# VectorE writes both bias tiles of a step, one comparison makes both one-hots, and a group's two additions are split over two steps

## The reference, cut to what matters

```
edge_feat = concatenate([x[src], x[dst], edge_attr])          # per edge
h         = mish(edge_feat @ W1 + b1)
messages  = mish(h @ W2 + b2)
agg       = segment_sum(messages, dst, num_segments=1250)
```

## Time and profile before

| | us |
|---|---|
| median of 3 runs | 1094.78 (1094.32 to 1095.49) |
| the profiled execution, own time | 1094.15 |
| its span | 1092.3 |
| busy in the span: PE / PEld / DVE / ACT / POOL | 1033.1 / 871.1 / 861.9 / 884.3 / 724.6 |

### The profile page before, as it was taken

One profiled execution on the slowest core, in us unless ns is written; L12 is line 12 of the kernel. 1 busy time (PEld: TensorE's weight loads), 2 busy tenths in 40 slices (PEclk: granted clock), 3 DMA queues, 4 the chain that ended last, 5 costly groups with the idle time before them and its releaser, 6 DMA issues.

```text
span 1092.3 us, 18562 instructions
## 1 busy us (share of the span) xinstructions
PE 1033.1 (95%) x5629; PEld 871.1 (80%) x5630; DVE 861.9 (79%) x1500; ACT 884.3 (81%) x1077; POOL 724.6 (66%) x626
## 2 busy tenths in 40 slices
PE   3558999999999999999999999999999999999997
PEld 1226889998889888888888888888888888888796
DVE  7998536635526389999999999999999999999686
ACT  6985735624503799999999999999999999999584
POOL 6875438745255587777777777777777777760227
PEclk8889999999999999999999999999999999999999
DMA  2005962674276387766676666667766666761002
GB/s 106 9 1 139 181 222 73 212 242 149 77 240 116 94 177 163 162 161 139 136 147 139 139 141 146 136 141 141 147 137 138 144 146 134 142 133 39 1 1 95
DMA packets 82914, 141.63 MB, mean 130 GB/s; under 512 B 11115, under 2 KB 39020, under 8 KB 82742
## 3 DMA queue, kind: packets, MB, share of 16 engines
q0 software_dynamic: 38048, 87.58, 40.1%
q1 hardware_dynamic: 44822, 53.52, 15.3%
HBM read 115.42 MB, written 20.39 MB: 124 GB/s over the span
## 4 chain that ended last, share of the span: by engine, by line
PE 85%; DVE 7%; ACT 2%; issue 2%; POOL 1%; DMA 1%; DVEq 1%; ACTq 0%; POOLq 0%
PE banks L1149 12%; PE banks L1150 12%; PE banks L1154 12%; PE banks L1047 10%; PE banks L1181 7%; PE banks L1131 7%; PE banks L1124 6%; PE banks L1091 5%; PE banks L965 4%; PE banks L1112 4%; DVE edge_counts L1823 2%; PE banks L1244 2%; DVE key_onehot L1762 1%; PE banks L1020 1%; PE banks L1147 1%
## 5 line engine op out<-in xcount | busy, mean ns | idle before, releaser
L798 POOL DMA_INDIRECT gather_pq<-q_table,dst x157 | 326.1, 2077 | 57.2 <-issue 47.5
L790 POOL DMA_INDIRECT gather_pq<-p_table,src x157 | 174.8, 1113 | 117.7 <-PE banks L1131 66.7
L1149 PE MATMUL banks<-w_lo,h_hi 128*128 128x512 f32 x620 | 242.0, 390 | 0.0
L1150 PE MATMUL banks<-w_hi,h_hi 128*128 128x512 f32 x620 | 241.8, 390 | 0.0
L1154 PE MATMUL banks<-w_hi,h_lo 128*128 128x512 f32 x620 | 166.0, 389 | 0.0
L1154 PEld LDWEIGHTS banks<-w_hi,h_lo 128*128 128x128 f32 x620 | 116.4, 188 | 24.4
L1150 PEld LDWEIGHTS banks<-w_hi,h_hi 128*128 128x128 f32 x620 | 116.4, 188 | 23.8
L1149 PEld LDWEIGHTS banks<-w_lo,h_hi 128*128 128x128 f32 x620 | 116.4, 188 | 23.3 <-issue 0.7
L2131 DVE SCALAR_TENSOR_TENSOR h_full<-mish_work,banks 128x512 f32<-128x512 f32 (+1 forms) x154 | 98.4, 681 | 45.1 <-ACT mish_work L1465 40.8
L2156 DVE SCALAR_TENSOR_TENSOR message<-mish_work,banks 128x1024 f32<-128x1024 f32 x78 | 95.3, 1222 | 8.4 <-ACT mish_work L1489 0.3
L1124 PE MATMUL banks<-ident,gather_pq 128*128 128x128 f32 x628 | 96.5, 275 | 1.4 <-DVE h_full L2131 0.8
(11 more groups left out here) (274 smaller groups left out, 2607.6 us busy)
## 6 DMA issues: line engine op xcount, KB each, us to landing
edge_attr<-in_edge_attr_t SPq DMA_DIRECT2D x20, 256.0 KB, 2.8
attr_high<-edge_attr_hi SPq DMA_DIRECT2D x40, 128.0 KB, 2.2
attr_low<-edge_attr_lo SPq DMA_DIRECT2D x40, 128.0 KB, 1.8
edge_attr_parts<-attr_high SPq DMA_DIRECT2D x79, 64.0 KB
edge_attr_parts<-attr_low SPq DMA_DIRECT2D x79, 64.0 KB
x_nodes<-h_hi POOLq DMA_DIRECT2D x10, 256.0 KB, 14.9
x_nodes<-h_lo POOLq DMA_DIRECT2D x10, 256.0 KB, 7.9
p_table<-p_stage SPq DMA_DIRECT2D x10, 256.0 KB, 2.0
```

The costliest lines, as they stand in the source:

```text
L790: nc.gpsimd.indirect_dma_start(GP[:, 2 * j + k, :], None, p_tab[:, :], bass.IndirectOffsetOnAxis(ap=SRC[:, 2 * s + k:2 * s + k + 1], axis= ...
L798: nc.gpsimd.indirect_dma_start(GP[:, 2 * j + k, :], None, q_tab[:, :], bass.IndirectOffsetOnAxis(ap=DST[:, 2 * s + k:2 * s + k + 1], axis= ...
L1149: pe.matmul(at, h_high(s, j)[:, c, e], W2_LO[:, c, :], start=False, stop=False, skip_group_check=True)
L1150: pe.matmul(at, h_high(s, j)[:, c, e], W2_HI[:, c, :], start=False, stop=False, skip_group_check=True)
```

## The change

Four edits, all in the edge loop:

1. `b2_both_tiles` takes the place of `b2_first_tile`: VectorE copies the bias to both Z2 banks of step s with one instruction of 1024 elements. ScalarE's `b2_second_tile` goes, and TensorE's product ones times bias in odd steps. One semaphore, `b2_seeded`, takes the place of two.
2. `hots1` is one `tensor_tensor` comparison of 256 elements in place of two `tensor_scalar` comparisons of 128.
3. The addition to the low block stays at the end of the even step. The addition to the next block moves into the odd step that follows, behind its two `full1`, together with the branch `more_of`.
4. `load_range` moves from the end of the even step to the odd step, behind `message`.

```diff
@@ TensorE, z2
-                if after(s, 2) and k == 0:
-                    pe.wait_ge(b2_first, s - 1)
-                elif after(s, 2) and j == 0:
-                    pe.wait_ge(b2_second, s)
+                if after(s, 2):
+                    if k == 0:
+                        pe.wait_ge(b2_seeded, s - 1)
                 else:
                     pe.matmul(at, ONES_R[:, :], B2_R[:, :], start=True, stop=False, skip_group_check=True)
@@ ScalarE
-            def b2_second_tile(s, j):
-                nc.scalar.copy(Z2[:, 2 * j + 1, :], B2_ROW[:, 0, :]).then_inc(b2_second, 2)
...
-                if j == 1 and after(s, 3) and live(s - 1) and tiles(s - 1) == 2:
-                    b2_second_tile(s - 1, 1 - j)
...
-            act.wait_ge(b2_in, 16)
@@ VectorE
-                make_hots([ONEHOT[:, j, k, :] for k in range(2)], REL_G, 2 * s).then_inc(hot_ready, 1)
+                wide = [P, 2, P]
+                nc.vector.tensor_tensor(ONEHOT[:, j, :, :], IOTA[:, 0:P].rearrange("p (o k) -> p o k", o=1).broadcast_to(wide),
+                                        REL_G[:, bass.ds(2 * s, 2)].rearrange("p (t o) -> p t o", o=1).broadcast_to(wide),
+                                        ALU.is_equal).then_inc(hot_ready, 1)
...
-            def b2_first_tile(s, j):
+            def b2_both_tiles(s, j):
                 dve.wait_ge(msg_full, s - 1)
-                nc.vector.tensor_copy(Z2[:, 2 * j, :], B2_ROW[:, 0, :]).then_inc(b2_first, 1)
+                nc.vector.tensor_copy(Z2[:, 2 * j:2 * j + 2, :], B2_ROW[:, :, :].broadcast_to([P, 2, DIM])).then_inc(b2_seeded, 1)
...
+            def group_low(s, n, group, bank):
                 wait_extras()
                 dve.wait_ge(agg_done, SUMS1 + group)
                 dve.wait_ge(seg_done, s + 1)
-                add_sums(n, group, bank).then_inc(agg_done, 1)
+                add_low(n, group, bank)
+
+            def group_next(s, group):
+
+                add_next(0, group, SEG[:, 0, :]).then_inc(agg_done, 1)
+                more_of(s, 0, group + 1)
...
             def edge_step(s, j, i):
 
                 if live(s):
                     for h in range(2):
                         full1(s, h)
+                if j == 1 and live(s - 4):
+                    group_next(s - 4, i - 2)
...
                 if live(s - 2):
                     message(s - 2, j)
+                if j == 1 and live(s - 3):
+                    load_range(0, i - 1)
                 if live(s - 2):
                     hots1(s - 2, j)
                     if live(s):
-                        b2_first_tile(s, j)
+                        b2_both_tiles(s, j)
                 if live(s):
                     lo1(s, j)
                 if live(s - 3):
-                    sums1(s - 3, i - 2 + j, j == 0)
-                if live(s - 2) and j == 0:
-                    load_range(0, i - 1)
+                    if j == 0:
+                        group_low(s - 3, 0, i - 2, SEG[:, 0, :])
+                    else:
+                        more_of(s - 3, 0, i - 1)
@@ VectorE, behind the last step
+            group_next(FINAL - 3, EDGE_GROUPS - 3)
+            load_range(0, EDGE_GROUPS - 2)
             hi2(FINAL - 2)
```

More of the change, by code:

```diff
@@ L418, in gnn_kernel @@
         h_full = [sem(f"h_full_{h}") for h in range(2)]
-        z2_done, b2_in, b2_first, b2_second = (sem(n) for n in ("z2_done", "b2_row_in", "b2_in_first_tile", "b2_in_second_tile"))
+        z2_done, b2_in, b2_seeded = (sem(n) for n in ("z2_done", "b2_row_in", "b2_in_both_tiles"))
         b_exp, b_sq, b_ln, b_r, msg_full, msg_hi, msg_lo = (sem(n) for n in
@@ L1505, in edge_step @@
                     sq2(s - 2)
-                if j == 1 and after(s, 3) and live(s - 1) and tiles(s - 1) == 2:
-                    b2_second_tile(s - 1, 1 - j)
-                if live(s - 2):
                     log2(s - 2)
@@ L1682, in node_tile, with add_low, add_next @@
                 return AGG[:, bass.ds(nt, 1), :].rearrange("p o d -> p (o d)")
[L1684 to L1690, removed]
+            def add_low(n, row, bank):
+                at = node_tile(low_tile(n))
+                nc.vector.scalar_tensor_tensor(at, bank, FROM_LOW[:, bass.ds(row, 1)], at, ALU.mult, ALU.add)
+            def add_next(n, row, bank):
+                at = node_tile(dve.snap(range_regs[n][R_NEXT], min_val=0, max_val=NT - 1))
+                return nc.vector.scalar_tensor_tensor(at, bank, BELOW_LOW[:, bass.ds(row, 1)], at, ALU.mult, ALU.add)
             def sums_extra(n, rel, tile, hots, bank, added):
@@ L2170, in lo2 @@
                 nc.vector.tensor_tensor(MSG_LO[:, :, :], MSG[:, :, :], MSG_HI[:, :, :].bitcast(F32), ALU.subtract).then_inc(msg_lo, 1)
-            def add_group(s, n, group, bank):
+            def group_low(s, n, group, bank):
                 wait_extras()
@@ L2177, in add_group @@
                 dve.wait_ge(seg_done, s + 1)
-                add_sums(n, group, bank).then_inc(agg_done, 1)
+                add_low(n, group, bank)
+            def group_next(s, group):
+                add_next(0, group, SEG[:, 0, :]).then_inc(agg_done, 1)
+                more_of(s, 0, group + 1)
+            def add_group(s, n, group, bank):
+                group_low(s, n, group, bank)
+                add_next(n, group, bank).then_inc(agg_done, 1)
             def more_of(s, n, added):
                 sums_extra(n, REL_G, 2 * s, [XHOT_R[:, k, :] for k in range(tiles(s))], SEG[:, 1, :], SUMS1 + added)
[L2183 to L2189, removed]
             def edge_step(s, j, i):
```

## The result

The changed kernel takes 1111.45 us in the median (1110.47 to 1113.96, 4 runs), the kernel before 1095.02 beside it. The ratio is 1.0154, 95% interval 1.0135 to 1.0173: slower by 1.5%. The profiled execution took 1110.63 with a span of 1108.8; before it was 1094.15 and 1092.3.

A forecast was written before the change was run, and what follows sets the result against it. A loop through VectorE, TensorE and ScalarE was taken to set 16.74 us a pair; after the change the odd seed's loop, 5.88 + 1.22 + 0.13 + 4.85 + 5.11 = 17.19, adds 16.2 over 36 pairs, less 0.5: 1110, range 1100 to 1119.

The forecast's parts named there:

- a loop through VectorE's even step: Edge loop before the change: VectorE, TensorE and ScalarE in turn set the pair at 16.74 us; 16.15 after the change.
- TensorE's own need: Edge loop: TensorE alone would need 16.66 us a pair before, 16.43 without its bias product of 0.23.
- the loop of the odd seed: From an odd step's full1 through bias copy, TensorE and exp1 to the next odd full1: 16.04 us before, 17.19 after.
- The copy: VectorE's bias copy of 1024 elements into PSUM: bounds 0.69 and 1.22 us, 1.22 taken, 0.53 more in each step.
- The one-hots: VectorE's one comparison of 256 elements for two: 0.34 us from start to start, gain 0.05 a step, bounds 0 and 0.15.
- The register load: VectorE's 0.75 us load in the odd step: taken as hidden beside the message of 1.22, with 0.1 allowed.
- The number of pairs: Odd steps from 5 to 77: 36 pairs, 16.2 us more in all; -0.5 ahead of the first stall.
- VectorE's own order: VectorE's instructions in the changed edge loop without its idle time: 16.44 us a pair, so not what binds.
- A sign that came only half: Profile after: full1 of both steps starts as inv1 ends, VectorE idle in both; ScalarE's share falls to some 93.
- A fast copy: Rival A, bias copy: 1024 elements take 0.69 us, loop 16.66, pair 0.08 shorter, time 1092; chance 0.08.
- a hidden seed: Rival B, odd step: TensorE doesn't wait for the seed and decides; pair 16.44 us, time 1084; chance 0.09.
- a late register load: Rival C, odd step: load isn't hidden behind the message and holds the one-hots back; up to 1138 us; chance 0.11.

The follow-up runs named there:

- the kernel with the old seeds: Changed kernel, but bias written as before: VectorE tile 0, ScalarE tile 1 of even steps, TensorE's product in odd steps; 1094.30 us, ratio to before 0.9994.
- the cut copy: Changed kernel with the odd steps' wide bias copy in two, tile 1 behind lo1 with its own semaphore; 1096.21 us, ratio to before 1.0007.
- the other two kernels: Changed kernel with an extra 256-element comparison ahead of the even copy, 1112.38 us; changed kernel with one-hots behind the copy, 1103.54 us.

## Why the prediction was right

The forecast was 1110 with a range of 1100 to 1119; measured were 1111.45, and 1110.63 in the profiled execution against 1109.9. By its steps:

- **The limits before.** That TensorE's fullness hid a loop through VectorE's even step stands: with that loop shortened, in the kernel with the old seeds, the wait of line 1124 goes and the pair falls by only 0.03. TensorE's own need was put at 16.66, and about 16.65 comes out of that kernel; what holds it at 16.71 is the loop of the odd seed, 0.06 above it.
- **The copy** measures 1.220 over the loop, the upper bound that was taken. By the Trainium skill ("VectorE: DVE Perf Modes", "What auto-detection actually checks") the doubled rate for a single fp32 source needs both the source and the destination in SBUF. The trace agrees for the wide form too: 1.220 into PSUM, against 0.69 for the cast of 1024 inside SBUF.
- **The one-hots** take 0.33 from start to start (610.77 to 611.10), 0.34 was taken; their mean is 0.418.
- **The register load** is hidden: message to one-hots is 1.14 us in odd steps, with the load beside it (609.63 to 610.77), and 1.13 to 1.14 in even ones.
- **The loop of the odd seed**: 5.88, 1.22, 0.13, 4.85, 5.11 were forecast; 5.86, 1.22, 0.12, 4.88, 5.10 are there. 17.19 against 17.18 in the pair shown and 17.15 in the mean of 35.
- **The number of pairs** was right in effect: 14.6 us in 35 pairs (0.42 each, against 0.45), and 1.9 outside, where -0.5 was put down. Two small errors of opposite sign; what lies in the 1.5 us behind step 77 I have not taken apart.
- **VectorE's own order** was put at 16.44. In the timeline of the changed kernel odd to even `full1` takes 8.31 without a wait for another engine, where its starts in the kernel before, with the additions, copies and comparison put in, give 7.93 - 0.86 + 0.67 + 0.53 - 0.05 = 8.22. The even `full1` also waits for the signal of `lo1`, the instruction just ahead of it, and sits idle for 0.10 there, which the term left out. The expectation of the cut copy, which takes the idle time and gaps off the whole pair, has 16.64. So the term was too small by 0.1 to 0.2; it didn't decide.
- **A sign that came only half.** `full1` of both steps was to start as `inv1` ends, with VectorE idle ahead of both. In odd steps it does so, 0.03 behind `inv1` and after 0.39 of idle. In even steps it starts 0.13 behind `inv1`, held by `lo1` as said. So VectorE had less room than forecast. ScalarE's share fell to 94.6, where some 93 was named.
- **The rivals.** A fast copy is excluded by 1.220, a hidden seed by 38 waits, a late register load by 1.14. The idle time of the weight load is 0.86 in the mean, inside the 0.6 to 0.9 that was named.

## What to carry to other kernels

When several engines show 90% and more, a busy share says nothing of what an added instruction costs. Follow one signal round to itself, through every engine that it passes, and count what stands between its two ends: here the same 0.34 us a pair cost 13.5 us of time in one place of VectorE's order and in two others nothing clear of the noise (0.9 and 1.2). And an instruction that does two jobs signals both at the end of the second; if someone waits for the first, two instructions can be faster, as they were here by 15.2 us, than the one they were merged into.

## What was not expected of the hardware

VectorE's casts of 1024 elements inside SBUF take 0.69 us in the kernel before and in the changed one; between 450 and 950 us none of their 120 and 116 is over 0.70. In the kernel with the cut copy 16 of 120 are over 0.72, up to 0.89. Two in a row, VectorE first, GpSimd's gathers in the same stretch below:

```profile
610.36 0.73 DVE L2171 CAST message_hi<-message 128x1024 fp32r<-128x1024 f32 x1
611.01 0.89 DVE L2137 CAST h_hi<-h_full 128x1024 fp32r<-128x1024 f32 x1
```

```profile
607.67 2.39 POOL L798 DMA_INDIRECT gather_pq<-q_table,dst  x1 [0.30 <-issue]
610.36 1.62 POOL L798 DMA_INDIRECT gather_pq<-q_table,dst  x1 [0.30 <-issue]
```

The long casts lie beside such a gather for 0.88 us in the mean, the others for 0.29. That they meet is seen; that the one slows the other is not shown, and in the kernel before casts beside gathers (0.56 us in the mean) stayed at 0.69. Long casts also stand in the kernels with the seeds as before (56 of 120 over 0.72), with the extra comparison ahead of the odd copy (49 of 114) or behind it (29 of 116), with the additions back (13 of 118) and with both tiles in even steps only (12 of 120); in the other two kernels none is. They aren't free: they account for most of the 0.07 on the seed's stretch in the kernel with the old seeds, and fit the pair of the kernel with the extra comparison ahead of the odd copy being 0.05 longer than the comparison alone explains.
